# Expert tiles between the last pairs of a gated attention and mixture-of-experts block

## The reference

```python
x = x + tanh(g_xattn) * xattn(layernorm(x), ctx)      # 16 heads of 64, layer norms with gain and bias inside
h = layernorm(x)
logits = h @ router_w                                 # 14 experts
e = argmax(logits);  weight = softmax(logits)[e]
hid = gelu(h @ w1[e] + b1[e])                         # 128 -> 256, exact Gelu
out = x + tanh(g_ffn) * weight * (hid @ w2[e] + b2[e])
```

## Time and profile before

| | us |
|---|---|
| median of 3 runs (lowest, highest) | 824.04 (823.38, 824.54) |
| profiled execution, its own time | 822.65 |
| span of that execution, first to last instruction | 820.9 |
| TensorE busy (share of the span) | 742.8 (90%) |
| VectorE busy | 584.0 (71%) |
| ScalarE busy | 570.9 (70%) |
| GpSimd busy | 487.0 (59%) |
| mean granted clock of TensorE | 0.949 of full speed |

### The profile page before, as it was taken

The page is one execution under the profiler, slowest core; times in us unless marked ns, Lnnn a source line. Parts: engine busy times, 40 slices in busy tenths (PEclk is TensorE's granted clock), DMA queues, the critical chain, the costliest instruction groups (busy, mean ns, idle before and its releaser), DMA issues. The chain is left out here.

```text
span 820.9 us, 34983 instructions
## 1 busy us (share of the span) xinstructions
PE 742.8 (90%) x12705; PEld 686.2 (84%) x12706; DVE 584.0 (71%) x1580; ACT 570.9 (70%) x1180; POOL 487.0 (59%) x1071
## 2 busy tenths in 40 slices
PE   6779999999999999999999999999999771888881
PEld 5569999999999999999999999999999661788881
DVE  5356678777877787787877777878877734577771
ACT  3667777787877777878778777777787521566660
POOL 2544566656666666666656666666666533477774
PEclk8999999999999999999999999999999865799996
DMA  4840011101010001110111101000000000655530
GB/s 124 251 120 20 20 34 33 31 30 30 30 30 30 30 30 37 35 32 30 37 35 32 36 30 30 30 30 30 21 22 23 29 20 26 173 155 148 149 99 1
DMA packets 50525, 43.90 MB, mean 53 GB/s; under 512 B 14632, under 2 KB 46026, under 8 KB 50474
## 3 DMA queue, kind: packets, MB, share of 16 engines
q1 hardware_dynamic: 43898, 30.53, 13.5%
q0 software_dynamic: 5632, 12.67, 4.4%
q10 hardware_dynamic: 944, 0.01, 0.1%
HBM read 28.55 MB, written 15.68 MB: 54 GB/s over the span
## 5 line engine op out<-in xcount | busy, mean ns | idle before, releaser
L450 POOL TENSOR_TENSOR probs<-probs,row_inv 128x1024 f32<-128x1024 f32 x64 | 122.0, 1907 | 46.9 <-DVE row_inv L1066 46.1
L570 ACT ACTIVATE KT<-psJ 128x512 f32<-128x512 f32 x128 | 76.2, 595 | 55.0 <-PE psJ L742 52.0
L1061 DVE TENSOR_REDUCE row_sum<-probs 128x16 f32<-128x1024 f32 x64 | 77.7, 1215 | 38.7 <-ACT probs L616 38.7
L610 ACT ACTIVATE PTs<-psT 128x512 f32<-128x512 f32 x128 | 75.9, 593 | 36.9 <-PE psT L836 36.9
L1074 DVE TENSOR_TENSOR OT_l<-psO,OT_h 128x1024 fp32r<-128x1024 f32 x64 | 78.1, 1221 | 24.7 <-ACT OT_h L603 24.7
L570 ACT ACTIVATE V<-psJ 128x512 f32<-128x512 f32 x128 | 73.2, 598 | 25.1 <-PE psJ L742 21.8
L616 ACT ACTIVATE probs<-probs 128x1024 f32<-128x1024 f32 x64 | 67.8, 1059 | 24.2 <-DVE probs L1053 24.1
L1046 DVE TENSOR_REDUCE row_max<-psS 128x16 f32<-128x1024 f32 x64 | 75.6, 1181 | 10.2 <-PE psS L799 10.2
L836 PE MATMUL psT<-ident,probs 128*128 128x128 f32 x512 | 79.3, 277 | 3.2 <-POOL probs L450 2.4
L740 PE MATMUL psJ<-XT_h,Wq_h 128*128 128x256 f32 x256 | 77.8, 304 | 3.1 <-ACT QT L570 3.0
L740 PE MATMUL psJ<-CT_h,Wk_h 96*128 96x256 f32 x256 | 77.8, 304 | 3.1 <-ACT QT L570 2.5
(11 more groups left out here) (202 smaller groups left out, 2185.4 us busy)
## 6 DMA issues: line engine op xcount, KB each, us to landing
V<-rows_by_expert SPq DMA_DIRECT2D x40, 129.0 KB
QT<-rows_by_expert SPq DMA_DIRECT2D x40, 129.0 KB, 2.3
x_in<-in_x_dram SPq DMA_DIRECT2D x32, 128.0 KB, 2.1
x_res<-in_x_dram SPq DMA_DIRECT2D x32, 128.0 KB, 2.1
c_in<-in_ctx_dram SPq DMA_DIRECT2D x32, 96.0 KB, 2.2
rows_by_expert<-pad_row SPq DMA_DIRECT2D x1, 1806.0 KB, 12.0
w_sb<-in_L_ffn_w_dram SPq DMA_DIRECT2D x1, 1792.0 KB, 8.5
rows_by_expert<-rows,place_i POOLq DMA_INDIRECT x64, 2.6
```

Of the source, the lines that this page charges most:

```text
L450: pool.tensor_tensor(pr, pr, row_inv[:, p.k % 2, :].unsqueeze(2).to_broadcast([P, 16, SEQ]), ALU.mult).then_inc(s_norm, 1)
L570: act.activation(dst, psJ[n % 2][:, :], ACT.Copy).then_inc(s_jobev, 1)
L610: act.activation(PTs[:, (p.k - 1) % 2, half, :], psT[:, :], ACT.Copy).then_inc(s_ptev, 1)
L1061: dve.tensor_reduce(row_sum[:, :], pr, AX.X, ALU.add).then_inc(s_sum, 1)
```

## The change

The first 32 tiles are taken from the counts after 28 groups. `first_table` fills them with whole tiles of 128 rows that are already there; it runs on VectorE in step 62 and is written out in step 63. What an expert has beyond its tiles so used goes into a second table (`last_table`), which has 45 tiles; 77 in all. The eight steps after step 63 are written out by hand on each engine, and the first 32 tiles stand between their pieces, two or four steps of `ffn` at a time; they are straight code, and the rest has a loop of two trips and 13 tiles of straight code. PSUM: since the last pieces need psM, psT and psO, the tiles use `psJ[0]` for the transpose, `psJ[1]` for W2 and the two banks of `psS` for W1. The rows of a tile have buffers in the old QT and KT, the outputs a buffer of their own. The roots of the last two groups (`last_roots`) are on VectorE. SyncE starts the loads when the scores of pair 63 are done and the rows of 28 groups have landed. GpSimd waits for the landing of the first 32 outputs before its loop.

```diff
--- before.py
+++ after.py
@@ -60,7 +60,10 @@
     PAIRS = TOK // P
     REGION = P + TOK
     ROW = D + D + 2
-    TILES = -(-(TOK // P + E - 1) // RING) * RING
+    FIRST = 2 * RING
+    KNOWN = GROUPS - 4
+    TILES = FIRST + (TOK - FIRST * P + E * (P - 1)) // P
+    assert (KNOWN * GT - E * (P - 1)) // P >= FIRST and 4 * RING <= TILES < 5 * RING
...
         w1_tile = [KTf[:, 4 * P + F * i:4 * P + F * (i + 1)] for i in range(4, 8)]
-        half = [Vf, QTf]
-        tile_rows = [half[i // (RING // 2)][:, ROW * (i % (RING // 2)):ROW * (i % (RING // 2) + 1)] for i in range(RING)]
-        at = ROW * RING // 2
-        tile_out = [half[i // (RING // 2)][:, at + D * (i % (RING // 2)):at + D * (i % (RING // 2) + 1)] for i in range(RING)]
+        spare = 4 * P + 8 * F
+        tile_rows = [QTf[:, ROW * i:ROW * (i + 1)] for i in range(RING - 1)] + [KTf[:, spare:spare + ROW]]
+        out_ring = sb("out_ring", [P, RING, D])
+        tile_out = [out_ring[:, i, :] for i in range(RING)]
...
-            for u in range(LOOP_TO, STEPS_U):
+            for u in range(LOOP_TO, GROUPS // 2):
                 for k in range(4):
                     step(Plan(u, k))
+        D64, D65, D66, D67, D68, D69 = (Plan(GROUPS // 2 + n // 4, n % 4) for n in range(6))
...
+        class First:
+            def __init__(self, eng, engine, ffn):
+                self.eng, self.engine, self.ffn, self.words, self.t = eng, engine, ffn, None, 0
+            def tiles(self, count):
+                for t in range(self.t, self.t + count):
+                    v, i = t // RING, t % RING
+                    if t == 0:
+                        self.words = [None] + list(entries(self.engine, expert_tab, 0, RING // PACK, 2 ** 16 - 1))
+                    elif i == 0:
+                        self.words = entries(self.engine, expert_tab, v * (RING // PACK) - 1, RING // PACK + 1, 2 ** 16 - 1)
+                    self.ffn(t, v, i, [t - n >= 0 for n in range(5)], experts(self.eng, self.words, i))
...
+        def rest(eng, engine, ffn):
+            with eng.Fori(FIRST // RING, 4) as v:
                 words = entries(engine, expert_tab, v * (RING // PACK) - 1, RING // PACK + 1, 2 ** 16 - 1)
                 for i in range(RING):
-                    ffn(v * RING + i, v, i, [True] * 5, experts(words, i))
-            words = entries(engine, expert_tab, TILES // PACK - 1, 1, 2 ** 16 - 1)
-            for i in range(4):
-                ffn(TILES + i, TILES // RING, i, [i - n < 0 for n in range(5)], experts(words, i))
+                    ffn(v * RING + i, v, i, [True] * 5, experts(eng, words, i))
+            words = entries(engine, expert_tab, 4 * (RING // PACK) - 1, RING // PACK + 1, 2 ** 16 - 1)
+            for t in range(4 * RING, TILES + 4):
+                ffn(t, t // RING, t % RING, [t - n < TILES for n in range(5)], experts(eng, words, t - 4 * RING))
...
+            sp.wait_ge(s_qk, PAIRS)
+            sp.wait_ge(s_pad, 32)
+            sp.wait_ge(s_scat[0], 32 * ((KNOWN + 1) // 2))
+            sp.wait_ge(s_scat[1], 32 * (KNOWN // 2))
+            sp.wait_ge(s_row_tab, 1)
+            for v in range(FIRST // RING):
+                load_trip(v, RING)
             for i in range(2):
                 sp.wait_ge(s_scat[i], 32 * (GROUPS // 2))
...
+            sp.wait_ge(s_row_tab, 2)
+            with sp.Fori(FIRST // RING, 4) as v:
+                load_trip(v, RING)
+            load_trip(4, TILES - 4 * RING)
...
-            with pool.Fori(0, TILES // RING) as v:
+            def tiles(first, count):
+                for t in range(first - 4, first - 4 + count):
+                    if t >= 0:
+                        send_out(t, t % RING)
+            send(D65)
+            tiles(4, 4)
+            send(D67)
+            tiles(8, 6)
+            send(D69)
+            tiles(14, FIRST - 14)
+            for t in range(FIRST - 4, FIRST):
+                send_out(t, t % RING)
+            for i in range(RING):
+                pool.wait_ge(f_scat[i], 16 * (FIRST // RING))
+            with pool.Fori(FIRST // RING, 4) as v:
...
-                act.wait_ge(s_newton, NEWT * (p.g + 2))
+                if p.fixed and p.g >= GROUPS:
+                    bias, scale = shift4[p.g - GROUPS][:, 0:2], rstd4[p.g - GROUPS][:, 0:2]
+                    act.wait_ge(s_rootx, 13 * (p.g - GROUPS + 1))
+                else:
+                    bias, scale = shift[:, 4:6], rstd[:, 4:6]
+                    act.wait_ge(s_newton, NEWT * (p.g + 2))
...
                     act.wait_ge(f_t1, t + 1)
-                    act.activation(n2_T[i % 4], psJ[i % 2][:, 0:P], ACT.Copy).then_inc(f_t1ev, 1)
+                    act.activation(n2_T[i % 4], psJ[0][:, 0:P], ACT.Copy).then_inc(f_t1ev, 1)
...
+            early = First(act, mybir.EngineType.Activation, ffn)
+            values_high(D64)
...
             act.wait_ge(s_b1, 1)
             act.wait_ge(s_tab, 1)
-            ffn_run(act, mybir.EngineType.Activation, ffn)
+            early.tiles(2)
+            route_exp(D64)
+            probs_out(D64, 0)
+            probs_out(D64, 1)
+            values_high(D65)
+            norm_x2(D65)
+            early.tiles(2)
+            norm_T(D65)
+            attn_out(D65)
+            early.tiles(2)
+            route_exp(D66)
+            early.tiles(2)
+            norm_x2(D67)
+            early.tiles(2)
+            norm_T(D67)
+            early.tiles(2)
+            route_exp(D68)
+            early.tiles(FIRST - 12)
+            act.wait_ge(s_tab, 2)
+            rest(act, mybir.EngineType.Activation, ffn)
...
+            def table(bank, n):
+                pe.wait_ge(s_cols, 3 * n)
+                for i in range(2):
+                    last = pe.transpose(bank[0:1, P * i:P * i + P], t_cols[:, i:i + 1], ident[:, :])
+                last.then_inc(s_tabT, 1)
             def step(p):
                 if p.k == 0:
@@ -904,6 +973,9 @@
                     if p.fixed and p.s == 1:
                         pe.wait_ge(s_wl, 4)
                     scores(p)
+                    if p.fixed and p.s == PAIRS - 1:
+                        pe.wait_ge(s_jobev, 12 * GROUPS)
+                        table(psJ[1], 1)
...
-                    if not (isinstance(t, int) and t < 2):
-                        pe.wait_ge(f_t1ev, t - 1)
+                    if not (isinstance(t, int) and t < 1):
+                        pe.wait_ge(f_t1ev, t)
                     pe.wait_ge(f_load[i], 16 * (v + 1))
-                    pe.transpose(psJ[i % 2][:, 0:P], tile_rows[i][:, D:2 * D], ident[:, :]).then_inc(f_t1, 1)
+                    pe.transpose(psJ[0][:, 0:P], tile_rows[i][:, D:2 * D], ident[:, :]).then_inc(f_t1, 1)
...
-                        last = pe.matmul((psM, psT)[i % 2][:, P * k:P * k + P], w1_tile[(i - 2) % 4][:, P * k:P * k + P],
+                        last = pe.matmul(psS[:, 512 * (i % 2) + P * k:512 * (i % 2) + P * k + P], w1_tile[(i - 2) % 4][:, P * k:P * k + P],
...
-                    if not (isinstance(t, int) and t < 6):
-                        pe.wait_ge(f_sum, t - 5)
+                    if not (isinstance(t, int) and t < 5):
+                        pe.wait_ge(f_sum, t - 4)
                     for k in range(FK):
-                        last = pe.matmul(psO[:, o:o + D], hid_T[i % 4][:, P * k:P * k + P],
+                        last = pe.matmul(psJ[1][:, 0:D], hid_T[i % 4][:, P * k:P * k + P],
                                          w2_sb[:, bass.ds(at[k], D)], start=(k == 0), stop=(k == FK - 1))
...
+            early = First(pe, mybir.EngineType.PE, ffn)
+            value_sums(D64)
+            post_a(D64)
...
+            pe.wait_ge(s_sub, PAIRS)
+            pe.transpose(psS[:, 0:E * FK], b1_rows[:, :], ident[0:E * FK, 0:E * FK]).then_inc(s_b1T, 1)
...
             pe.wait_ge(s_tab, 1)
-            ffn_run(pe, mybir.EngineType.PE, ffn)
+            early.tiles(2)
+            router(D64)
+            probs_T(D64, 0)
+            probs_T(D64, 1)
+            rank(D64)
+            value_sums(D65)
+            early.tiles(2)
+            post_b(D65)
+            out_proj(D65)
+            early.tiles(2)
+            post_a(D66)
+            router(D66)
+            early.tiles(2)
+            rank(D66)
+            early.tiles(2)
+            post_b(D67)
+            early.tiles(2)
+            router(D68)
+            early.tiles(2)
+            rank(D68)
+            early.tiles(4)
+            misc_free()
+            table(psM, 2)
+            early.tiles(FIRST - 18)
+            pe.wait_ge(s_tab, 2)
+            rest(pe, mybir.EngineType.PE, ffn)
...
-                dve.wait_ge(s_newton, NEWT * (p.g + 1))
+                if p.fixed and p.g > GROUPS:
+                    dve.wait_ge(s_rootx, 13 * (p.g - GROUPS))
+                else:
+                    dve.wait_ge(s_newton, NEWT * (p.g + 1))
...
+            def last_roots(p):
+                i = p.g - GROUPS
```

(93 more changed lines are left out.)

98 lines of the change are left out of this document (49 added, 49 removed).

## The result

The changed kernel takes 856.12 us (median of 4 runs, 854.71 to 859.69), the kernel before 823.71 (822.79 to 824.54): ratio 1.0397, 95% interval 1.0377 to 1.0418, slower by 32.4 us. The forecast was 858. The profiled execution took 859.69 for a span of 857.8, so it lies 3.6 above its median. Group lines of its page, to be read beside the table of the profile before and the earlier trace rows (the sends); columns: busy us, mean ns of one, idle before and what ended most of it.

The account below looks back on a forecast made before the run. TensorE and GpSimd both bound the old tile stage; W2's one-bank ring would slow it. Tile 32 at 757, plus 60.0 + 30.0 + 1.3 + 8.4, gave a span of 856.7 us; forecast 858, range 823 to 874.

Parts of the forecast that it names:

- The ring: W2's single bank psJ[1]: weight load to sum, sum and release were put at 1.66 us a tile, against 1.00.
- A trip of 30.0: One 16-tile trip of TensorE's loop was put at 30.0 us, for 20.87 before.
- First table: VectorE between pair 62's and pair 63's subtractions: table steps, TensorE cooling and writing out were put at 3.6 us together.
- Last pairs: Pair 63's value sums to group 31's output projection: sums put at 675.1, projection's end at 691.2, before 676.3.
- The queueing term: Waits added ahead of group 31's projection: 2.2 + 2.6 + 1.3 + 1.2 = 7.3 us.
- the roots save 2.3 each, and the queueing gives it back: Last two groups' roots on VectorE: 2.6 us for GpSimd's 4.95, a saving that queueing ahead of the projection returns.
- From there to tile 32: Group 31's projection to tile 32's transpose: 40.8 us to 732.0, then 13 W2, issue and words, to 757.
- the 2.6 for two table loads: ScalarE, group 31's Exp between Gelus: two table loads were put at 2.6 us on the path.
- B: Rival: address work done before the wait, so the ring is 1.27 us and the time 831; chance 0.20.
- D: Rival: TensorE falls to half clock in the ring's pauses, ring 2.1 us and time 889; chance 0.08.
- C: Rival: tiles fill the attention stage's idle end, GpSimd's 1.29 us is the only pace, time 812; chance 0.12.
- (E): Rival: gains and costs of the change cancel, within 0.2%; chance 0.03.

Follow-up runs that it names:

- The first experiment: Changed kernel with W2 again taking the two banks of psO in turn for all 77 tiles: 822.19 us, ratio 0.9978 to the kernel before.
- the second: Changed kernel with W2 reading its weights from one fixed address, still one bank: 840.80 us, ratio 1.0195 to the kernel before.
- The ninth experiment: Changed kernel with 16 more dependent small VectorE steps on scratch behind the first table: 858.88 us, ratio 1.0445 to the kernel before.
- experiment 3: Changed kernel with the roots of the last two groups back on GpSimd: 853.00 us, ratio 1.0349 to the kernel before.
- experiments 4: Changed kernel with two banks for W2 and transposes alternating between psJ[0] and psJ[1]: 820.82 us, ratio 0.9954 to the kernel before.
- 5: Changed kernel with two banks for both W2 and transposes, and the last two groups' roots on GpSimd: 815.31 us, ratio 0.9900 to the kernel before.
- 6: Kernel with both bank pairs and roots on GpSimd, plus group 31's projection and its eviction moved ahead in the TensorE and ScalarE queues: 816.62 us, ratio 0.9910.
- experiment 8: Changed kernel with the last two groups' exponentials using Gelu's table, so four table loads go: 859.39 us, ratio 1.0420 to the kernel before.
- experiment 1: Changed kernel with W2 back on the two banks of psO, waiting for the sum of two tiles before: 822.19 us, ratio 0.9978 to the kernel before.

## Why the forecast held, step by step

**The ring.** Forecast 0.93 + 0.29 + 0.44 = 1.66 us; measured 0.93 + 0.29 + 0.43 = 1.65. The release had been read in the tail of the old trace, where W2 waits for a sum; in the steady trip of that trace it waits for none. Taking the bare handoff for it would have given 1.27. A trip of 30.0 came out as 30.4. The first experiment shows the bank as cause, the second the address as the larger part of the release (0.31 of 0.43 us).

**First table.** Forecast 3.6 on the path. Pair 62's to pair 63's subtraction was 653.74 - 643.32 = 10.42 us and is 660.60 - 646.34 = 14.26: 3.8. The ninth experiment shows that this stretch has no cover. The timeline of the changed kernel, table steps from first to last, the residual behind them, and TensorE waiting for it:

```profile
647.48 0.16 DVE L1294 TENSOR_TENSOR n_tiles<-next_row,r_int 128x14 f32<-128x14 f32 x1
...
650.15 0.17 DVE L1331 TENSOR_TENSOR skip<-skip,full 128x14 f32<-128x14 f32 x1
650.72 0.43 DVE L1183 TENSOR_TENSOR rows<-psM,x_res 128x256 f32<-128x256 f32 x1 [0.39 <-DVE skip L1331]
```

```profile
651.20 1.04 PE L943 MATMUL psM<-rw_sb,n2T 128*128 128x14 f32 x4 [4.10 <-DVE rows L1183]
```

**Last pairs.** Pair 63's value sums were put at 675.1 and start at 678.14, less 3.0 for the opening: 675.1. The end of group 31's projection was put at 691.2; its last part runs from 692.51 for 1.61 us, to 694.12, less 3.0: 691.1. To agree to 0.1 us is in part luck: in the trace of experiment 3, whose program is the same up to there, the value sums start 28.83 us after pair 62's subtraction, in the changed kernel's 31.80. The queueing term (7.3 forecast, 15.98 - 8.85 = 7.1 measured) is right in size, and in its parts: from the value sums to the end of the projection experiments 4, 5 and 6 take 15.84, 11.18 and 8.62 us. So the roots on VectorE are 4.7 of it (2.2 + 2.6 forecast), and what stands ahead in the queues 2.6 (1.3 + 1.2). What the forecast had wrong here is a sentence, not the sum: "the roots save 2.3 each, and the queueing gives it back" puts their move at about nothing, and it costs 4 to 5 us (experiments 3 and 5). It set durations against each other, 2.6 and 4.95 us, and not the start: on VectorE the roots begin 9.75 us after their means are done (672.63 to 682.38).

**From there to tile 32.** Forecast 40.8 us to the end of the second table, measured 694.12 to 732.47, 38.35. The term that was too large is the 2.6 for two table loads: by experiment 8 this stretch takes 38.35 us without its four loads as well, and 40.8 less 2.6 is 38.2. From 732.47 to tile 32's transpose at 757.34 it is 24.9, as forecast (13 ring steps and the words); from there to the end of the span 100.5, forecast 99.7. The whole span, less 3.0, is 854.8 for the 856.7 of the sum.

**Table loads and the page.** In the changed kernel an activation follows 0.01 to 0.02 us behind a load, and without four loads the stretch that held them was as long as before. The Trainium skill (ScalarE: Activation LUTs, What ACT_TABLE_LOAD costs) adds a drain of about 1.38 us to each; nothing of it can be seen here.

**The rivals.** B (1.27 us, 831) needed the address to be ready before the wait; the entries of the line still follow it. With a fixed address the ring is 1.34 us, so B had the size of the ring without that work nearly right. D (half clock, 889) needed a granted clock near 0.5 in the trips. The windows give 0.91 to 0.96, mostly the upper of the two levels (2.4 GHz), with TensorE busy for 13.5 to 16.3 of 20 us. Between 760 and 780 the kernel with two banks was granted 0.83, so a lower clock is not tied to the single bank. The Trainium skill (TensorE: Matmul & The Clock Gate, A second HAM failure mode: psum-queue depth-cycling) tells of such a fall; it did not come here. C (GpSimd as the only pace, 812) comes close in time to the kernel without the ring and with the roots back on GpSimd, 815.31, but its mechanism holds there only for the last 44 intervals; in the 32 before, 1.78 us each, something else is the pace. Its condition, a ring under 1.15 us, fits: at 1.00 GpSimd is the pace of the last 44, at 1.34 it isn't (66.46 us, 1.51 each). (E), a cancelling of gain and cost, is nearly experiment 1, at 0.9978. So what is left of the change without the bank and the roots is worth 8 to 9 us (814.93 and 815.31 against 823.05 and 823.94 of the kernel before in the same comparisons), and the bank that it gave up for W2 cost four times as much, 33.9. The 8 to 9 us are not the overlap alone: there are also three tiles fewer, 3.9 us at GpSimd's 1.29 (an estimate), and no run separates the two.

**What stays open.** Why executions whose opening is the same get a different granted clock between 20 and 100 us; what paces the first 32 tiles once both banks are back and the roots are on GpSimd; and how the 38.35 us split into their terms one by one, apart from the table loads.

## What to carry to other kernels

When an edit gives work earlier at the price of a buffer, count the ring that the last buffer closes: producer, consumer, release, with the release read where the trace really shows that wait, and multiply it by every step it governs. Before giving a buffer up, look where its last old user stands in the order of the engine that wants it: here that was ahead of the first new use. A step that has been moved to a faster engine is only earlier if that engine is free when the step's inputs are; compare the start, not the duration. Align two executions at a point where both still do the same work, and measure small effects from there.

## What was not expected of the hardware

- A table load of ScalarE runs ahead of the wait of the activation that needs it (load at 696.59, 4.10 us of waiting, activation at 701.97). Without the four loads of 1.28 us the stretch that held them took the same 38.35 us.
- The weight load behind a satisfied wait starts 0.12 us after the releasing sum's end with a fixed address and 0.43 with one computed from a table; the ring is 1.34 us and 1.65.
- TensorE, idle for 0.2 to 0.5 us ahead of most W2, one every 1.65, kept a granted clock of 0.91 to 0.96 over the trips. Two other stretches differ from trace to trace at the same program: the opening, granted 0.89 to 0.98 (3.0 us between two profiled runs), and step 63, granted 1.00 in experiment 3's trace and 0.50 in the changed kernel's (3.05 us up to tile 0's transpose).
